# Expert outputs scattered to token rows from inside the expert loop and added in two passes of plain loads; the tile copy made on ScalarE

## What is computed

```python
scores = jax.nn.softmax(t @ gate_w.T, axis=-1)
weights, indices = jax.lax.top_k(scores, TOP_K)          # 16 experts, TOP_K = 2
y = jnp.zeros_like(t)
for e in range(N_EXPERTS):
    w_e = jnp.sum(jnp.where(indices == e, weights, 0.0), axis=-1)
    y = y + _swiglu(t, w1[e], w3[e], w2[e]) * w_e[:, None]
z = _swiglu(t, sw1, sw3, sw2)
...
x = x + tanh(g_ffn[1]) * (y + z)
```

## Time and profile before

| what | us |
|---|---|
| three runs | 1027.53, 1028.21, 1030.4 (median 1028.21) |
| the profiled execution | 1029.54 |
| its span, first to last instruction | 1028.0 |
| TensorE matmuls busy | 961.9 (94%) |
| VectorE, ScalarE, GpSimd busy | 461.5, 262.8, 94.0 |
| longest stretch at the end without TensorE | from 996.4 to 1028.0 |

### The profile page before, as it was taken

How to read it: one execution, slowest core, us unless ns; L and a number is a source line. 1 busy time by engine, 2 the same in 40 slices (tenths; PEclk the granted TensorE clock), 3 DMA queues, 4 the chain that set the end, 5 groups by cost and what they waited for, 6 DMA issues and landing times.

```text
span 1028.0 us, 16990 instructions
## 1 busy us (share of the span) xinstructions
PE 961.9 (94%) x7151; PEld 735.3 (72%) x7152; DVE 461.5 (45%) x703; ACT 262.8 (26%) x403; POOL 94.0 (9%) x121
## 2 busy tenths in 40 slices
PE   5999999999999999699999999989999999999970
PEld 5878788787878887599995458978985455555530
DVE  6665455455445457951211648974414111121114
ACT  4542333323333235131211204332210011111100
POOL 0000000000000020100000012120002412111115
PEclk9999999999999999799999999998799999999995
DMA  8000000010100021330003009117003329887416
GB/s 318 31 2 32 11 22 32 1 32 1 73 2 31 2 83 43 134 154 1 1 1 122 1 20 360 40 47 252 3 1 135 123 71 321 287 278 244 166 41 214
DMA packets 25874, 95.92 MB, mean 93 GB/s; under 512 B 3282, under 2 KB 4306, under 8 KB 22738
## 3 DMA queue, kind: packets, MB, share of 16 engines
q1 hardware_dynamic: 18338, 69.02, 19.0%
q0 software_dynamic: 7472, 25.96, 7.2%
HBM read 76.35 MB, written 18.61 MB: 92 GB/s over the span
## 4 chain that ended last, share of the span: by engine, by line
PE 86%; DVE 7%; ACT 2%; issue 2%; POOL 1%; DMA 1%; POOLq 0%; DVEq 0%; ACTq 0%
PE ps L520 17%; PE ps L521 16%; PE ps L522 16%; PE ps L912 10%; PE ps L781 6%; PE ps L922 6%; PE ps L600 4%; PE ps L888 4%; PE ps L583 3%; PE ps L801 1%; POOL arena L1776 1%; PE ps L903 1%; DVE stats L1249 1%; PE ps L929 1%; PE ps L622 1%
## 5 line engine op out<-in xcount | busy, mean ns | idle before, releaser
L520 PE MATMUL ps<-arena_r 128*125 128x512 f32 (+1 forms) x416 | 164.1, 394 | 3.1 <-DVE arena_r L1227 3.1
L521 PE MATMUL ps<-arena_r 128*125 128x512 f32 (+1 forms) x416 | 157.2, 378 | 0.0
L522 PE MATMUL ps<-arena_r 128*125 128x512 f32 (+1 forms) x416 | 156.9, 377 | 0.0
L520 PE MATMUL ps<-hT,arena_r 128*128 128x448 f32 (+1 forms) x368 | 138.7, 377 | 3.5 <-DVE hT L1268 3.3
L521 PE MATMUL ps<-hT,arena_r 128*128 128x448 f32 (+1 forms) x368 | 136.6, 371 | 0.0
L522 PE MATMUL ps<-hT,arena_r 128*128 128x448 f32 (+1 forms) x368 | 136.4, 371 | 0.0
L912 PE MATMUL ps<-arena 128*128 x336 | 103.1, 460 | 1.6 <-ACT arena L1196 1.0
L976 ACT ACTIVATE arena<-arena,mbias,mscale 125x448 f32<-125x448 f32 x96 | 66.2, 752 | 106.1 <-DVE arena L1349 106.1
L520 PEld LDWEIGHTS ps<-arena_r 128*125 128x125 f32 (+1 forms) x416 | 78.1, 188 | 20.8 <-issue 4.1
L522 PEld LDWEIGHTS ps<-arena_r 128*125 128x125 f32 (+1 forms) x416 | 78.0, 188 | 13.8
L912 PEld LDWEIGHTS ps<-arena 128*128 128x128 f32 x336 | 62.2, 190 | 33.2 <-issue 2.1
(11 more groups left out here) (187 smaller groups left out, 1205.6 us busy)
## 6 DMA issues: line engine op xcount, KB each, us to landing
arena<-in_e SPq DMA_DIRECT2D x16, 1408.0 KB, 6.5
arena<-in_e SPq DMA_DIRECT2D x16, 512.0 KB, 8.7
sorted_rows<-arena POOLq DMA_DIRECT2D x1, 7424.0 KB, 23.4
land_c<-in_ctx SPq DMA_DIRECT2D x8, 752.0 KB, 4.4
arena<-sorted_rows POOLq DMA_DIRECT2D x21, 256.0 KB, 6.3
sorted_rows<-arena POOLq DMA_DIRECT2D x21, 256.0 KB, 6.1
land_w<-in_gu SPq DMA_DIRECT2D x8, 512.0 KB, 4.4
arena<-in_e SPq DMA_DIRECT2D x16, 192.0 KB, 9.0
```

The source lines that it names most:

```text
L520: mm(into, a[0], w[0], start=i == 0, stop=False)
L521: mm(into, a[0], w[1], start=False, stop=False)
L522: last = mm(into, a[1], w[0], start=False, stop=i == len(operands) - 1)
```

## The change

Rows of `sorted_rows` become 514 values long: 512 of the token, then a row number and the router weight of the pair. The row number says where in a second DRAM tensor, `token_rows`, the pair's output goes: 128 spare rows, then a first block of 896 rows for the lower-numbered expert of each token and a second block for the higher one. Padding rows go to the spare rows. The loop multiplies by the weight in `tile_hidden`, and stores each output tile with an indirect DMA to `token_rows`. After the loop SyncE loads the first block and the second block with plain DMAs, and VectorE adds them in two passes. There is one output buffer (`yr`) where there were two. The copy to `xg` moves from GpSimd to ScalarE. Core of the diff:

```diff
+ROW = D + 2
-        A_YR = A_SH + 2 * D
+        yr = at(A_SH + 2 * ROW, D)
+        weight = at(A_TO + 8, 1)
+        y_dram = nc.dram_tensor("token_rows", (P + 2 * TOK, D), F32, kind="Internal").ap()
@@ sync, after the last expert's weights
+            last = sp.value_load(expert_end[0:1, NE - 2:NE - 1], ...)
+            tiles = sp.value_load(tile_count[0:1, 3:4], ...)
+            for j, landed in enumerate((last, tiles)):
+                sp.wait_ge(y_st, landed * 16)
+                for t in range(NT):
+                    first = P + j * TOK + t * P
+                    sp.dma_start(back[t][j], y_dram[first:first + P, :]).then_inc(back_ld[t][j], 16)
@@ scalar
+            def place(n):
+                act.wait_ge(xg_ld, n * 16 + 16)
+                if not (isinstance(n, int) and n == 0):
+                    act.wait_ge(xg_tr, n)
+                    act.wait_ge(row_read, n)
+                fn(xg, arena[:, bass.ds(A_XR + n % 2 * ROW, ROW)], ACT.Copy).then_inc(xs_rdy, 1)
+            place(0)
             rows_save(0)
-            with act.Fori(0, last1) as n:
+            place(1)
+            with act.Fori(0, last2) as n:
                 silu_tile(n)
                 rows_save(n + 1)
+                place(n + 2)
@@ vector
+            (six small operations after the router's weights: ends_of, row number and weight of each pair)
             def tile_hidden(n):
+                dve.wait_ge(row_read, n + 1)
-                v.tensor_tensor(hmoe[:, 0:EI], ps[:, 5, 0:EI], smoe, ALU.mult).then_inc(m_h, 1)
+                v.scalar_tensor_tensor(hmoe[:, 0:EI], ps[:, 5, 0:EI], weight, smoe, ALU.mult, ALU.mult).then_inc(m_h, 1)
+            def row_ends(n):
+                dve.wait_ge(xs_rdy, n + 1)
+                dve.wait_ge(m_h, n)
+                v.tensor_tensor(arena[:, bass.ds(A_TO + n % 4, 1)], xg[:, D:D + 1], lane[:], ALU.max)
+                v.tensor_copy(weight, xg[:, D + 1:ROW]).then_inc(row_read, 1)
-                v.tensor_scalar(arena[:, bass.ds(A_YR + (n % 2) * D, D)], ps[:, 3, :], 1.0, None, ALU.mult
+                v.tensor_copy(yr, ps[:, 3, :]).then_inc(d_sv, 1)
-            with dve.Fori(3, tiles) as n:
+            with dve.Fori(3, last1) as n:
                 tile_hidden(n)
-                tile_out(n - 1, n * 16 - 32)
+                row_ends(n + 1)
+                tile_out(n - 1, n * 16 - 16)
                 tile_hidden_save(n)
             for t in range(NT):
-                dve.wait_ge(back_ld[t], 32)
-                (two scalar_tensor_tensor with wtop, then out_st)
+                dve.wait_ge(back_ld[t][0], 16)
+                v.tensor_tensor(x[:, t, :], x[:, t, :], back[t][0], ALU.add).then_inc(back_add, 1)
+            for t in range(NT):
+                dve.wait_ge(back_ld[t][1], 16)
+                dve.wait_ge(back_add, t + 1)
+                v.tensor_tensor(x[:, t, :], x[:, t, :], back[t][1], ALU.add).then_inc(out_st, 1)
@@ gpsimd
             for j in range(2):
+                if j == 1:
+                    pool.wait_ge(scattered, 16 * NT)
+                nc.gpsimd.tensor_copy(h3_row[:, :, D:ROW], ends_of[:, j]).then_inc(ids_set, 1)
+                pool.wait_ge(ids_set, 2 + j)
                 (7 indirect scatters, as before)
+            def next_load(n):
+                pool.wait_ge(xg_ld, n * 16)
+                pool.wait_ge(xs_rdy, n - 1)
+                load(n)
+            def scatter(n, stored=None):
+                pool.wait_ge(d_sv, n + 1)
+                if stored is not None:
+                    pool.wait_ge(y_st, stored)
+                nc.gpsimd.tensor_copy(to_row[:], arena[:, bass.ds(A_TO + n % 4, 1)]).then_inc(to_set, 1)
+                pool.wait_ge(to_set, n + 1)
+                pool.indirect_dma_start(y_dram, bass.IndirectOffsetOnAxis(to_row[:, 0:1], 0), yr, None
+                                        ).then_inc(y_st, 16)
-            (load, place and store per turn)
+            with pool.Fori(5, tiles) as n:
+                next_load(n)
+                scatter(n - 3, n * 16 - 48)
-            for t in range(NT):
-                for j in range(2):
-                    pool.indirect_dma_start(back[t][j], None, xs_dram, dest[:, j, t:t + 1]) ...
```

More of the change, by code:

```diff
@@ L372, in flamingo @@
         y_st = sem("y_st")
+        xs_rdy = sem("xs_rdy")
+        ids_set = sem("ids_set")
+        ends_set = sem("ends_set")
+        row_read = sem("row_read")
+        to_set = sem("to_set")
+        to_held = sem("to_held")
+        back_add = sem("back_add")
         out_st = sem("out_st")
@@ L381, in flamingo @@
         e_ld = [sem(f"e_ld{i}") for i in range(NSLOT)]
-        back_ld = [sem(f"back_ld{t}") for t in range(NT)]
+        back_ld = [[sem(f"back_ld{t}_{j}") for j in range(2)] for t in range(NT)]
         block = stack.enter_context(nc.Block())
@@ L1579, in _ @@
             then(v.tensor_scalar(wtop[:], top8[:, :, 0:2], tg[:, 3:4], None, ALU.mult))
-            ids = iota16.unsqueeze(1).broadcast_to([P, NT, NE])
-            then(v.tensor_tensor(one0, ids, idxf[:, :, 0:1].broadcast_to([P, NT, NE]), ALU.is_equal))
-            then(v.tensor_tensor(one1, ids, idxf[:, :, 1:2].broadcast_to([P, NT, NE]), ALU.is_equal))
+            v.tensor_copy(ends_of[:, 0, :, 1], wtop[:, :, 0])
+            v.tensor_copy(ends_of[:, 1, :, 1], wtop[:, :, 1])
+            dve.wait_ge(ids_set, 1)
+            for j in range(2):
+                then(v.tensor_tensor(ends_of[:, j, :, 0], idxf[:, :, j], idxf[:, :, 1 - j], ALU.is_gt))
+                v.scalar_tensor_tensor(ends_of[:, j, :, 0], ends_of[:, j, :, 0], float(TOK), ids[:], ALU.mult, ALU.add
+                                       ).then_inc(ends_set, 1)
+            experts = iota16.unsqueeze(1).broadcast_to([P, NT, NE])
+            then(v.tensor_tensor(one0, experts, idxf[:, :, 0:1].broadcast_to([P, NT, NE]), ALU.is_equal))
+            then(v.tensor_tensor(one1, experts, idxf[:, :, 1:2].broadcast_to([P, NT, NE]), ALU.is_equal))
             then(v.tensor_tensor(both, one0, one1, ALU.add))
@@ L1657, in _ @@
             tile_hidden(2)
-            tile_out(1)
+            row_ends(3)
+            tile_out(1, 16)
             tile_hidden_save(2)
-            with dve.Fori(3, tiles) as n:
+            with dve.Fori(3, last1) as n:
                 tile_hidden(n)
-                tile_out(n - 1, n * 16 - 32)
+                row_ends(n + 1)
+                tile_out(n - 1, n * 16 - 16)
                 tile_hidden_save(n)
-            tile_out(last1, last2 * 16)
+            tile_hidden(last1)
+            tile_out(last2, last2 * 16)
+            tile_hidden_save(last1)
+            tile_out(last1, last1 * 16)
             for t in range(NT):
-                dve.wait_ge(back_ld[t], 32)
-                for j in range(2):
-                    last = v.scalar_tensor_tensor(x[:, t, :], back[t][j], wtop[:, t, j:j + 1], x[:, t, :],
-                                                  ALU.mult, ALU.add)
-                    if j == 0:
-                        then(last)
-                last.then_inc(out_st, 1)
+                dve.wait_ge(back_ld[t][0], 16)
[4 more added lines that the diff above has]
+                v.tensor_tensor(x[:, t, :], x[:, t, :], back[t][1], ALU.add).then_inc(out_st, 1)
         @block.gpsimd
```

88 lines of the change are left out of this document (39 added, 49 removed).

## The result

Over four runs the changed kernel takes 1013.85 us (1012.07 to 1014.8), the kernel before 1028.93 (1027.53 to 1030.4, four runs). The ratio is 0.9856, with a 95% interval of 0.9838 to 0.9875. The profiled execution of the changed kernel took 1014.06 us, its span is 1012.4. TensorE's matmuls are busy for 956.3 in place of 961.9, with the same 7151 instructions, and GpSimd for 82.2 in place of 94.0. Two of the runs of the kernel before that are counted further down took 1512 and 1902 us, were disturbed, and stand in no ratio.

The account below looks back on a forecast made before the run. TensorE bounds the kernel until its last matmul, then GpSimd's gather issue does (17.5 us). Landing at 1002.65 with the loop's 0.7, plus 11.5 and 1.5, ends the span at 1015.65, 12.4 less: median 1015.8, range 1012.5 to 1021.

Parts of the forecast that it names:

- Loop entry: Before the expert loop: scatter rounds and first load run later, hidden by 1.1 us of cover; 0, bounds 0 and 2.
- The copy on ScalarE: In loop turns: the moved copy, its wait and the weight multiply fit idle time; 0, bounds 0 and 0.1 per turn.
- One output buffer: In the loop: `tile_out` waits for the previous tile's landing, lagging 0.2 to 0.8 per loaded tile; 0.7, bounds 0 and 4.
- third rival: In the loop: scatters landing in 7.3 under load make the one buffer exceed its cover; total 1021, chance 0.07.
- The last tile: At the last tile: its `tile_out` waits for the scatter of the tile before; 0.2, bounds 0 and 1.
- The last scatter: After the last `tile_out`: copy 0.4, landing 2.7 in place of 2.31, adds beside it 0.4; landed at 1001.95.
- second rival: At the last scatter: GpSimd is shut out by all seven first-pass adds, 4.8 less 0.4 counted; total 1020.1, chance 0.07.
- The first block: Its loads and adds hide beside the last two tiles' work; cost 0, or 5.8 us without cover.
- The end: After the last landing: 17.5 us of gather issue removed; plain loads and stores take 11.5 at 319 GB/s plus 1.5 fixed.
- the sign: At the kernel's end: DMA at 300 GB/s or more in the last 12 us.
- first rival: At the end: loads and stores keep the old 215 GB/s whoever issues them; total 1021.3, chance 0.09.
- slower case: In the loop: scatters landing after 7.9 us make the one buffer cost the whole gain; 1030 to 1035, chance 0.03.

Follow-up runs that it names:

- place_act: The kernel before with only the copy to xg moved from GpSimd to ScalarE, stores and gathers unchanged: 1025.75 us, ratio 0.9965.
- reg_early: The kernel before with TensorE reading the expert number for its down product ahead of the wait for the copied rows, copy left on GpSimd: 1025.54 us, ratio 0.9972.
- after_again: The changed kernel run once more, unedited, beside the version with four edits at its end: 1011.64 us, ratio 0.9834 to the kernel before.
- last_free: The changed kernel with an own output buffer and early VectorE-made row numbers for the last tile, whose scatter waits only for its save: 1011.6 us, ratio 0.9831.
- after: The changed kernel itself, in its first profiled trace, against the kernel before: 1013.85 us, ratio 0.9856.
- one_wait: The changed kernel with the first block's loads held until all 21 outputs have landed: 1014.64 us, ratio 0.985.
- adds_late: The changed kernel with the first-pass adds held until the last scatter has landed: 1010.35 us, ratio 0.9823.
- last_buf: The changed kernel with an output buffer of its own for the last tile: 1014.71 us, ratio 0.9856.
- best: The changed kernel with own last-tile buffer, early row numbers, three second-block loads on ScalarE, first-pass adds held for the last scatter: 1010.9 us, ratio 0.9835.

## Why the prediction was right, step by step

The forecast was 1015.8 with a range of 1012.5 to 1021; measured 1013.85. The sum said 12.4 less span, the two profiles show 15.6, of which 2.5 lies before the loop, where the same kernel moves by 3.2. What remains, 13.1, is two errors of opposite sign: the end gave 1.6 less than the sum had, the loop 2.35 more. The mechanism of the end is as told; that the sum comes so near is in part luck.

*Loop entry.* Counted at 0, bounds 0 and 2. The first load was issued at 812.78 (forecast 814.2) and landed 3.09 later (3.2). ScalarE's copy ran from 815.89 to 816.52, TensorE began its transposes at 816.58, and had stood idle for 0.5: the shared expert was done sooner than in the trace of before, so the cover of 1.1 wasn't there. Within the bounds.

*The copy on ScalarE.* Here the prediction failed: "0, bounds 0 and 0.1 per turn". The copy's own work is hidden, as said. But taking it off GpSimd was worth 2.1 to 2.6 (place_act), and the bounds excluded a gain. The step that failed is the question I asked, who waits for the copy and whether it is in time, where the question was what stands in TensorE's queue behind that wait. The register read of 0.30 to 0.77 us needs to run while earlier products still keep TensorE busy. reg_early shows it. The chain's 0.31 of "issue" was there to be read.

*One output buffer.* The mechanism came as told. `tile_out` (L1697) is released by the landing in all 12 loaded turns, and once more at the last tile. Timeline of VectorE in the changed kernel, and the scatter's time to landing (min/median/max):

```profile
851.18 0.69 DVE L1697 COPY arena<-ps 128x512 f32<-128x512 f32 x1 [2.55 <-DMA token_rows<-arena,to_row]
...
860.70 0.69 DVE L1697 COPY arena<-ps 128x512 f32<-128x512 f32 x1 [3.99 <-DMA token_rows<-arena,to_row]
...
869.40 0.69 DVE L1697 COPY arena<-ps 128x512 f32<-128x512 f32 x1 [4.62 <-DMA token_rows<-arena,to_row]
...
877.25 0.69 DVE L1697 COPY arena<-ps 128x512 f32<-128x512 f32 x1 [4.39 <-DMA token_rows<-arena,to_row]
...
885.61 0.69 DVE L1697 COPY arena<-ps 128x512 f32<-128x512 f32 x1 [4.12 <-DMA token_rows<-arena,to_row]
...
893.07 0.69 DVE L1697 COPY arena<-ps 128x512 f32<-128x512 f32 x1 [3.50 <-DMA token_rows<-arena,to_row]
...
DMA to landing us min/median/max: 2.8/5.8/7.5
```

From one to the next it is 9.5, 8.7, 7.9, 8.4 and 7.5. With turns of 8.08, two tiles run later by 1.4 and 0.6, and then the lag shrinks while weights are still loaded: it limits itself, as said, and sooner. It does not grow by 0.2 to 0.8 a tile over six tiles. TensorE's 0.7 (0 to 4) came out at 0 to 1.1: the loop is 174.60 in after_again, as in last_free or place_act, and 175.70 in after, with two turns of 8.63 and 8.57. In both, ScalarE's copy of the late rows ends 0.2 before the transposes, and 0.28 and 0.23 of "issue" stand in front of the down product. That is the mark which reg_early takes away in the kernel before; reg_early's line in the changed kernel was not run. The longest landing, 7.5, even meets the condition of the third rival (7.3), but not its price; the median is 5.8, below the 6.1 of the stores before.

*The last tile.* Forecast 0.2, bounds 0 and 1. Measured: `tile_out` 1.51 after the last down product (2.10 in after_again) where it was 0.34, so 1.2 to 1.8. The term was mis-sized: the scatter it waits for lands in 3.7 to 4.3, not in 2.7. one_wait shows the cause, the first block's loads: without them `tile_out` starts 0.56 after the last down product, the 0.2 of the forecast. I had named them as the reason for the upper bound and then set it too low.

*The last scatter.* From `tile_out`'s end to the issue 1.46 (forecast 1.2 to 1.8); landing 3.01 (2.7, and 0.2 more of the issue beside the adds); the adds cost 0.40 in all (forecast 0.4), by adds_late. The rows also show what that 0.40 is. Seven adds of 0.69 in 4.29 begin 0.60 apart. The copy of the row numbers began 0.36 into an add and took 0.18 more than in adds_late; in last_buf it began 0.27 into an add (995.62, adds from 994.75) and took 0.28 more. The scatter's issue began 0.34 into an add and took 0.22 more; in last_free it began 0.28 into one (993.17, adds from 992.29) and took 0.28 more than in best. In all four, what had passed of the add and the delay make 0.54 to 0.56: GpSimd is held until the add in progress is nearly over, and not by those that follow. The Trainium skill (SBUF — State Buffer, "SBUF: two separate sides") has a VectorE instruction with two SBUF inputs and a GpSimd instruction that reads SBUF take a shared port pair in turn, each for its whole instruction. The trace agrees: at most one add per step, by 0.18 to 0.28 here, and nothing near the 4.4 of the second rival, which has all seven adds in front. From the last down product to the last landing the sum had 5.5; it was 6.7 (7.25 in after_again).

*The first block.* Its loads ran from 985.2, the adds from 994.40 to 998.69, ahead of the landing. Its own cost is 0, its side cost the 1.2 to 1.8 above. Without the cover I had 5.8; one_wait has 3.4 to 3.8 there.

*The end.* Forecast 13.0 (11.5 at 319 GB/s and 1.5 of fixed parts, so 282 GB/s over the whole of it); measured 13.45 and 13.85, at 280 GB/s over the 13.1 from the landing. Over the last 12.0 it is 302, as the sign had it. The first rival (17.1 at 215 GB/s and the 1.5, 18.6) is out. One reading of the old end was off: its 14 gathers' issues lie 1.30 apart on average, 16.9 from first to last, not 14 x 1.25; the forecast doesn't use that product.

So the end gave 11.5, where the sum had 13.1 without the loop's 0.7, and the loop gave 1.65 where the sum had a loss of 0.7. In the end, 1.15 of the missing 1.6 lie ahead of the last landing and 0.45 behind it. The slower case needed landings of over 7.9 turn after turn. The longest was 7.5, the median 5.8.

## What to carry to other kernels

When a semaphore wait of the busiest engine is met just in time, look at what its queue holds behind the wait: a register read there is exposed, though the data was in time, and moving the read ahead of the wait costs one line. A gain at the end of a kernel is to be measured from the last product to the span's end, not by the total, as long as what comes before it moves from run to run by more than the edit does, and even then a second trace of the same kernel has to say how far the end itself moves (1.0 here). A step hidden beside other transfers is not free if the critical transfer of the end runs among them: price the landing beside them, not alone.

## What was not expected of the hardware

- A read of one value into a register of TensorE takes 0.30 us where the one for the down product stands ahead of the wait (297 to 312 ns over 42 reads, reg_early), and up to 0.765 in the kernel before. In the changed kernel the longest is 0.553.
- An indirect scatter of 128 rows of 2 KB lands in 2.7 to 2.8 alone, in 3.0 when VectorE adds during its issue, in 3.5 to 4.3 beside seven plain loads of 256 KB, and in up to 7.5 in the loop (median of all 21 in the changed kernel: 5.8).
- The traffic of the end has a dip that I can't explain. GB/s in 40 slices of 998 to 1012, after first, then best:

```profile
GB/s 374 24 0 0 0 59 94 281 427 380 322 351 334 205 263 351 252 252 217 176 217 228 363 386 410 410 398 416 410 392 410 410 392 421 404 363 322 146 29 0
```

```profile
GB/s 0 0 70 82 152 187 369 398 398 416 404 363 369 404 380 427 404 380 398 386 410 375 410 404 392 392 421 381 398 410 369 141 0 0 0 0 0 0 0 0
```

The same 3.67 MB, at about 220 for 2 us in the one (1003.6 to 1005.7) and at about 400 throughout in the other. In best the first store is issued at 1002.87, when all loads have been issued for over 3 us. adds_late has a dip as well, from 999.4 to 1001.2, before its first store is issued at 1001.58, so loads and stores side by side are not what makes it. What does stays open.
